# A gather loop on GpSimd that issues in groups of three and waits for each group to land

## What is computed

```python
h = feat[src]
def step(m, rw):
    r, w_r = rw
    mask = jnp.where(etypes == r, 1.0, 0.0).astype(h.dtype)
    m = m + mask[:, None] * (h @ w_r)
    return (m, None)
m, _ = jax.lax.scan(step, m0, (jnp.arange(n_rels), weight))
out = jax.ops.segment_sum(m, dst, num_segments=feat.shape[0])
x = layernorm(x + out)
```

## Time and profile before

| what | value |
|---|---|
| timed runs | 767.06 us median of 3 (766.12 to 768.82) |
| profiled execution, span from first to last instruction | 1331.0 us (its own time beside the span is not given) |
| TensorE busy | 905.4 us |
| VectorE busy | 656.1 us |
| ScalarE busy | 628.9 us |
| GpSimd busy | 553.1 us |
| mean granted TensorE clock | 0.784 of full speed |
| DMA | 58.93 MB |

### The profile page before, as it was taken

How to read it: one execution, slowest core, us unless ns; L and a number is a source line. 1 busy time by engine, 2 the same in 40 slices (tenths; PEclk the granted TensorE clock), 3 DMA queues, 4 the chain that set the end, 5 groups by cost and what they waited for, 6 DMA issues and landing times.

```text
span 1331.0 us, 25286 instructions
## 1 busy us (share of the span) xinstructions
PE 905.4 (68%) x8746; PEld 801.7 (60%) x8747; DVE 656.1 (49%) x2201; ACT 628.9 (47%) x1217; POOL 553.1 (42%) x591
## 2 busy tenths in 40 slices
PE   4576686766766768676675857667676766767676
PEld 3465575665656657566565756557575655756575
DVE  7653644545545364453635445363544545354444
ACT  6455453553544535444453535445363444535442
POOL 5643534444434353343534344352533435344341
PEclk9687887877868688686887778786787778788676
DMA  6211211111111111111111111121111111111111
GB/s 166 54 45 37 53 40 39 42 46 42 43 36 46 33 51 42 38 45 34 49 40 41 38 41 43 34 51 28 53 41 36 45 34 51 35 44 43 28 28 35
DMA packets 29901, 58.93 MB, mean 44 GB/s; under 512 B 11656, under 2 KB 11906, under 8 KB 29882
## 3 DMA queue, kind: packets, MB, share of 16 engines
q0 software_dynamic: 18464, 37.85, 11.0%
q1 hardware_dynamic: 11264, 20.41, 5.8%
q10 hardware_dynamic: 154, 0.42, 0.1%
HBM read 56.23 MB, written 2.40 MB: 44 GB/s over the span
## 4 chain that ended last, share of the span: by engine, by line
PE 66%; issue 30%; ACT 2%; DVE 1%; DMA 0%; ACTq 0%; DVEq 0%
PE own L767 48%; PE agg L805 11%; PE rel L818 6%; ACT pick L426 1%; DVE outT L647 0%; DMA x_sb<-in_x 0%; ACT away L420 0%; PE rel L825 0%; PE own L915 0%; DVE x_sb L681 0%; ACT rows L436 0%; DVE xp L558 0%; PE own L748 0%; ACT idx L451 0%; DVE outT L622 0%
## 5 line engine op out<-in xcount | busy, mean ns | idle before, releaser
L767 PE MATMUL own<-xp,pick 125*128 125x192 bf16 x5725 | 653.5, 271 | 377.6 <-issue 371.3
L767 PEld LDWEIGHTS own<-xp,pick 125*128 125x128 bf16 x5725 | 545.9, 108 | 474.6 <-issue 458.6
L345 POOL DMA_INDIRECT rows<-x_parts,gidx x558 | 529.5, 949 | 612.5 <-ACT gidx L379 231.1
L539 DVE TENSOR_SCALAR pick<-src_h,node 125x516 bf16<-125x516 f16 (+1 forms) x1220 | 459.7, 456 | 291.5 <-ACT src_h L387 290.3
L435 ACT ACTIVATE rows<-own 128x384 bf16<-128x384 f32 x122 | 57.4, 470 | 643.0 <-remote 581.2
L622 DVE TENSOR_TENSOR outT<-outT,rel 64x32 f32 x124 | 22.3, 180 | 361.6 <-PE rel L825 349.2
L420 ACT ACTIVATE away<-src_h,node_neg 125x516 bf16<-125x516 f16 (+1 forms) x305 | 192.5, 693 | 7.6 <-PE own L767 5.9
L426 ACT ACTIVATE pick<-away,one 125x516 bf16<-125x516 bf16 (+1 forms) x305 | 192.0, 696 | 0.0
L805 PE MATMUL agg<-onehot,rows 128*128 128x112 bf16 x2418 | 167.9, 243 | 15.8 <-issue 15.6
L805 PEld LDWEIGHTS agg<-onehot,rows 128*128 128x128 bf16 x2418 | 163.7, 117 | 18.3 <-issue 18.1
L605 DVE TENSOR_SCALAR onehot<-ramp,krel 128x112 bf16<-128x112 bf16 x806 | 148.9, 262 | 6.6 <-PE agg L805 6.6
(11 more groups left out here) (67 smaller groups left out, 83.0 us busy)
## 6 DMA issues: line engine op xcount, KB each, us to landing
src_b<-in_src SPq DMA_DIRECT2D x61, 258.0 KB
rows<-x_parts,gidx POOLq DMA_INDIRECT x577
x_parts<-xp SPq DMA_DIRECT2D x1, 728.0 KB
x_parts<-xp SPq DMA_DIRECT2D x1, 672.0 KB
out<-x_sb SPq DMA_DIRECT2D x2, 224.0 KB
x_sb<-in_x ACTq DMA_DIRECT2D x1, 364.0 KB
x_sb<-in_x SPq DMA_DIRECT2D x1, 336.0 KB
src_i<-in_src SPq DMA_DIRECT2D x1, 312.0 KB
```

Of the source, the lines that this page charges most:

```text
L345: pool.indirect_dma_start(rows[:, u, j, :], None, x_parts, bass.IndirectOffsetOnAxis(ap=gidx[:, u, j:j + 1], axis=0)).then_inc(rows_in[u] ...
L539: v.tensor_scalar(pick[u][:, b, 0:CUT * cut_width(u, odd)], src_h[u][:, :, 0:cut_width(u, odd)], node[:, b:b + 1], None, ALU.is_equal).the ...
L767: return nc.tensor.matmul(own_slot(u, h), pick[u][:, b, h * P:(h + 1) * P], xp[:, b, 0:SPLIT, :].rearrange("p s d -> p (s d)"), start=(b = ...
```

## The change

`fetch` on GpSimd gets further waits. A small function `gather` holds the indirect DMA that stood three times. Ahead of a fetch GpSimd waits until the last three gathers (tiles 10 to 12) of the fetch before, which belong to the other half, have landed. Within a fetch it waits after tile 6 until the gathers so far have landed, and again after tile 9 (`BREAKS`). In the first turn of half 1, which has three more gathers, it waits for these too. Nothing else is touched.

```diff
+    BREAKS = (7, LATE)
...
+            def gather(s, u, j):
+
+                pool.indirect_dma_start(
+                    rows[:, u, j, :], None, x_parts,
+                    bass.IndirectOffsetOnAxis(ap=gidx[:, u, j:j + 1], axis=0)).then_inc(s, 16)
+
             def fetch(i, u, odd):
                 if not is_first(i):
                     pool.wait_ge(agg_ready[u], i)
                 pool.wait_ge(gidx_ready[u], i + 1)
+
+                if u == 1:
+                    pool.wait_ge(late_in[0], (i + 1) * (16 * (GT - LATE)))
+                elif not is_first(i):
+                    pool.wait_ge(late_in[1], i * (16 * (GT - LATE)))
                 pool.nop(nofuse=True)
                 if not has_own(i, u):
                     for j in range(FEWER):
-                        pool.indirect_dma_start(
-                            rows[:, u, j, :], None, x_parts,
-                            bass.IndirectOffsetOnAxis(ap=gidx[:, u, j:j + 1], axis=0)).then_inc(first_in, 16)
+                        gather(first_in, u, j)
+                    pool.wait_ge(first_in, 16 * FEWER)
                 if own_count(u, odd) == FEWER:
-                    pool.indirect_dma_start(
-                        rows[:, u, FEWER, :], None, x_parts,
-                        bass.IndirectOffsetOnAxis(ap=gidx[:, u, FEWER:FEWER + 1], axis=0)).then_inc(fourth_in, 16)
+                    gather(fourth_in, u, FEWER)
                 for j in range(OWN[u], GT):
-                    pool.indirect_dma_start(
-                        rows[:, u, j, :], None, x_parts,
-                        bass.IndirectOffsetOnAxis(ap=gidx[:, u, j:j + 1], axis=0)).then_inc(rows_in[u] if j < LATE else late_in[u], 16)
+                    gather(rows_in[u] if j < LATE else late_in[u], u, j)
+
+                    if j + 1 in BREAKS:
+                        pool.wait_ge(rows_in[u], i * (16 * (LATE - OWN[u])) + 16 * (j + 1 - OWN[u]))
+                        pool.nop(nofuse=True)
```

## The result

The changed kernel takes 1141.81 us (median of four runs, 1141.67 to 1142.87), the kernel before 767.94 us in runs on the same chip: a ratio of 1.4878, 95% interval 1.4855 to 1.4902. Slower, as forecast; 1083 us was the forecast, so the time is 59 us above it and inside the range of 944 to 1150.

The account below looks back on a forecast made before the run. The prediction took the timed kernel as a never-waiting chain of GpSimd gathers (sum 762.7 us). It added 186 waits x (1.25 + 0.75 - 0.30 = 1.70 us) = 316 us to 767, giving 1083 us; range 944 to 1150 us.

Parts of the forecast that it names:

- TensorE's starvation: TensorE idle 371.3 us in the recorded 1331.0 us execution; most of it claimed absent from the timed runs.
- 186 waits, none of them covered: On GpSimd: 124 inside fetches, 61 ahead of fetches, 1 in turn 0, each directly after the gathers it waits for.
- Landing 1.25 us: Part (a) of a wait: from the end of a group's last gather instruction to its landing, 1.25 us.
- Restart 0.75 us: Part (b) of a wait: from the release to GpSimd's next gather start, 0.75 us.
- The step of 0.30 us that falls away: Part (c): the usual step between two GpSimd gathers, 0.30 us, subtracted from each wait's 1.70 us price.
- The transfer of source numbers: Holds up a landing to 1.88 us; at most one wait of three meets it, 39 us more, 1122 us.
- Nothing gained from a shorter queue: GpSimd's gathers get no cheaper with fewer in flight: 0.94 us after 10 us of rest, as for the ninth.
- Cheaper waits: Rival: the recording stretches the 0.75 us restart; 0.95 to 1.4 us a wait, 944 to 1027 us; chance 0.22.
- shorter gathers: Rival: the 0.30 us step is the recorder's, another engine sets 767 us; 907 us; chance 0.07.
- TensorE at half clock as the bound: Rival: resting TensorE drops to half clock, 19.9 us a turn, 1275 us; chance 0.03.
- Landing of 2.17 us counted from the instruction's end: Rival: landing takes 2.17 us after the gather instruction's end, 2.62 us a wait, 1254 us; chance 0.03.
- Faster or even: Rival: pauses between groups let TensorE be fed, at best 719 us; chance 0.03 faster, 0.02 just even.

Follow-up runs that it names:

- the second recording: The kernel before, unchanged, profiled again: span 766.3 us, timed 768.22 us.
- the run with 558 waits: The changed kernel with a wait after each gather of tiles 4 to 11, not each third: 1933.05 us (one run).
- the one that looks back one group: The changed kernel with 184 waits in place of its own, each for the group before the last: 767.96 us, ratio 1.0007 to the kernel before.

## Why the prediction was right, and where it was off

- **That GpSimd's chain bounds the timed kernel**, read out of a trace that showed something else: right. Shown by one gather more (77.1 us for 77.5 forecast by the same price), by the second recording, and by the sum of 762.7 us against a span of 766.3.
- **TensorE's starvation as something of the recorded execution**: right for the timed runs, and shown by the second recording. What caused it is open. It wasn't seen again, and that in the stretches read it ended with the landing of the last gather is no cause yet.
- **186 waits, none of them covered**: right. The trace has 186 pauses of more than 2.1 us, each from the issue of a group to behind its landing.
- **Landing 1.25 us: the term that was mis-sized.** The last packet does end 1.25 us after the instruction in the mean. But the term stood for the time until GpSimd is released, and the semaphore's update comes another 0.34 us later, 1.59 us after the instruction. The sum had nothing for these 0.34 us.
- **Restart 0.75 us**: right, 0.74 us from the update. I had taken it from GpSimd's restarts after the end of a ScalarE instruction (and, in the row from 1289.62 to 1290.40, of a TensorE instruction, though the text calls it an index list's), and it holds after a DMA's update too. **The step of 0.30 us that falls away**: right, 0.31 us. Together the wait is 0.32 us dearer than 1.70, and 0.32 us x 186 = 60 us is the miss of 59 us.
- **The transfer of source numbers**: I had bounded it at one wait in three. In the changed kernel its packets overlap 20 of 186 landings (4 of the 8 from 1.40 us up), and cutting it down saves 7 us; where the wait ahead of a fetch is gone, they overlap 57 of 125, and cutting it down saves 32 us. So the bound was of the right kind, and its size hangs on where the transfer falls against the wait.
- **Nothing gained from a shorter queue**: right, by the run with 558 waits and by the one that looks back one group.
- **The rivals.** Cheaper waits and shorter gathers are out: the restart is 0.74 us in the recorded execution of the changed kernel too, which was not stretched, and the gathers cost 1.243 us in the timed runs. TensorE at half clock as the bound is out: the mean clock fell to 0.833 and stretches of 0.50 appear, but TensorE waits 304 us for rows. Landing of 2.17 us counted from the instruction's end is out: even the update comes at 1.59 us. Faster or even is out.
- **The recorded span of about 1540 us** was wrong, since it was built on the stretched 1331 us. It was 1141.1 us.

## What to carry to other kernels

A wait for what an engine has just issued costs it the landing, the semaphore's update and the restart each time, here 2.01 us on the engine that sets the pace; nearly as many waits for the group before the last issued cost nothing. If the flow has to be held back, look back by more issue time than a wait costs (here three gathers, 3.7 us, against 2.0 us; a shorter look back was not run). Where a recorded execution is far from the timed ones, add up each engine's work against the timed median, and record again before reading a bottleneck out of it. And when a wait for a DMA is priced, count it up to the semaphore's update (a row of the chain view, or the time to landing in the view of a line) and not to the last packet; the restart is then that of the waiting engine.

## What was not expected of the hardware

- The semaphore's update comes 0.34 us after a gather's last packet (mean of 170 waits; 0.30 to 0.35 us for eight in ten).
- From the same update at 608.65, ScalarE takes 0.12 us to its next instruction, TensorE 0.13 us and GpSimd 0.74 us; GpSimd's 0.74 us are the same to 0.01 us in eight of ten of the 170 waits.
- Of the 2.50 us from a gather's start to the update, 1.65 us pass before its first packet, 0.51 us are packets and 0.34 us follow the last one.
- Two recorded executions of one kernel had spans of 1331.0 and 766.3 us, with the timed ones at 767 us throughout.
